# Three full attentions: turned probabilities as the weights of the value products, sums from a ones column, division by token, result turned afterwards

## The reference, cut to what matters

```python
def _L3_xcond_ref(q, k, v, tau, delta, Wq, bq, Wk, bk, Wv, bv, Wo, bo):
    qh = (q @ Wq.T + bq).reshape(B, L, H, E)
    kh = (k @ Wk.T + bk).reshape(B, S, H, E)
    vh = (v @ Wv.T + bv).reshape(B, S, H, E)
    scores = jnp.einsum('blhe,bshe->bhls', qh, kh)
    scores = scores * tau[:, None, None, :] + delta[:, None, None, :]
    a = jax.nn.softmax(scale * scores, axis=-1)
    out = jnp.einsum('bhls,bshd->blhd', a, vh).reshape(B, L, D)
    return out @ Wo.T + bo
...
x = x + _L3_xcond_ref(_layernorm(x, axis=-1), ctx_1024, ctx_1024, condB_tau[:, None], fside_BxS2_0, ...)
```

## Time and profile before

| | us |
|---|---|
| median of 3 runs | 3504.17 (3503.16 to 3506.55) |
| the profiled execution's own time | 3504.71 |
| its span, first to last instruction | 3503.0 |
| TensorE busy | 3144.3 (90%) |
| VectorE busy | 2451.7 (70%) |
| ScalarE busy | 1078.8 (31%) |
| GpSimd busy | 940.4 (27%) |

### The profile page before, as it was taken

How to read it: one execution, slowest core, us unless ns; L and a number is a source line. 1 busy time by engine, 2 the same in 40 slices (tenths; PEclk the granted TensorE clock), 3 DMA queues, 4 the chain that set the end, 5 groups by cost and what they waited for, 6 DMA issues and landing times. The chain is left out here.

```text
span 3503.0 us, 67687 instructions
## 1 busy us (share of the span) xinstructions
PE 3144.3 (90%) x27654; PEld 2380.6 (68%) x27670; DVE 2451.7 (70%) x6457; ACT 1078.8 (31%) x1919; POOL 940.4 (27%) x1000
## 2 busy tenths in 40 slices
PE   5998999897699756577799999999999997999999
PEld 4776766565477623366688888888888885777444
DVE  5787355001577799844688888888888884778666
ACT  3444211221344344444322222222222212444000
POOL 2332000232243200000144434434435343333000
PEclk9999999999799977788799999999999997999999
DMA  3100210343300000021200000000000002010000
GB/s 124 38 26 16 81 50 13 88 115 77 111 26 26 11 1 1 22 68 38 97 1 1 1 1 1 1 1 1 2 1 1 2 1 75 26 38 2 13 19 18
DMA packets 81171, 108.26 MB, mean 31 GB/s; under 512 B 11744, under 2 KB 62176, under 8 KB 80480
## 3 DMA queue, kind: packets, MB, share of 16 engines
q1 hardware_dynamic: 74720, 95.40, 8.3%
q0 software_dynamic: 6144, 8.52, 1.3%
HBM read 87.00 MB, written 16.91 MB: 30 GB/s over the span
## 5 line engine op out<-in xcount | busy, mean ns | idle before, releaser
L2035 POOL TENSOR_TENSOR pk_hisig<-pk_hihot,pk_sigs 128x512 f16<-128x512 f16 x512 | 520.6, 1044 | 668.3 <-DVE pk_hihot L2242 667.4
L2096 PE MATMUL pk_ps<-pk_nt,ew_downT 128*128 128x128 f32 x4096 | 515.5, 279 | 0.0
L2096 PEld LDWEIGHTS pk_ps<-pk_nt,ew_downT 128*128 128x128 f32 x4096 | 479.7, 192 | 15.3 <-issue 15.3
L2137 PE MATMUL pk_ps<-ew_up,pk_act_h 128*128 128x256 f32 x2048 | 450.4, 381 | 0.9 <-DVE pk_act_h L2230 0.9
L2137 PEld LDWEIGHTS pk_ps<-ew_up,pk_act_h 128*128 128x128 f32 x2048 | 388.8, 191 | 53.1 <-issue 1.0
L2043 ACT ACTIVATE pk_act_h<-pk_ps 128x512 f32<-128x512 f32 x256 | 153.0, 597 | 542.3 <-PE pk_ps L2096 542.3
L2243 DVE TENSOR_TENSOR pk_lohot<-pk_iota_h,pk_ps 128x1024 f16<-128x1024 f16 x256 | 312.1, 1219 | 0.0
L568 DVE RECIPROCAL a_rden<-a_ps_o 128x256 f32<-128x256 f32 x96 | 168.4, 1754 | 159.9 <-PE a_ps_o L458 159.9
L557 DVE TENSOR_REDUCE a_mx<-a_ps_s 128x8 f32<-128x1024 f32 x192 | 226.1, 1219 | 54.4 <-PE a_ps_s L432 54.3
L273 ACT ACTIVATE a_pT<-a_ps_t 128x512 f32<-128x512 f32 x384 | 209.0, 599 | 145.8 <-PE a_ps_t L441 145.6
L2416 PE MATMUL mo_ps<-mw_we,mo_xnT 128*128 128x512 f32 x512 | 225.6, 599 | 0.0
(11 more groups left out here) (353 smaller groups left out, 5433.5 us busy)
## 6 DMA issues: line engine op xcount, KB each, us to landing
ro_w<-in_L_W SPq DMA_DIRECT2D x16, 1024.0 KB, 7.1
a_ctx_t<-in_ctxT SPq DMA_DIRECT2D x24, 512.0 KB, 3.8
a_tau<-in_tau SPq DMA_DIRECT2D x24, 256.0 KB, 4.1
a_delta<-in_delta SPq DMA_DIRECT2D x24, 256.0 KB, 4.3
X<-in_x SPq DMA_DIRECT2D x4, 1024.0 KB, 9.5
row_dram<-sh_row SPq DMA_DIRECT2D x8, 512.0 KB, 3.2
sum_dram<-sh_new SPq DMA_DIRECT2D x8, 512.0 KB, 2.9
X<-sum_dram SPq DMA_DIRECT2D x4, 1024.0 KB, 9.6
```

The lines of the kernel that those rows point to most:

```text
L2035: ins = pool.tensor_tensor(hisig[:, buf, n, :, :, :], hi, sig2.broadcast_to([P, TP, 2, ECH]), ALU.mult)
L2096: ins = pe.matmul(hid.bank(f"h{c}")[:, j * P:(j + 1) * P], downT[:, k, e * P:(e + 1) * P], nt[:, s, k, :], start=(k == 0), stop=(k == KC - 1))
L2137: ins = pe.matmul(tail.bank("y")[:, 0:D], act_h[:, s, c, :], up[:, c, :], start=(c == 0), stop=(c == ECH - 1))
```

## The change

In the three attentions `weighted_values` exchanges its operands. The turned probabilities of one head, 128x128, are now the weights, and the head's values with a column of ones behind them, 17 columns, move. There are 16 products a tile in place of 32, into one bank with a row for each token and 17 columns for each head: 16 results and the sum. `divide` takes the reciprocal of 128x16 sums and multiplies with it broadcast over a head's 16 columns, into the new tile `o`, token by feature. Since `output_rows` needs features on partitions, `o` is turned by two transposes (`turn_out`) into one of the two banks `ps_t`, and ScalarE copies them out to `oT` (`out_columns`). These two stand one slot later, between the first m piece and `turn_probs(t, 2)` on TensorE, and between the emptying of the first m piece and `exps(t, 2)` on ScalarE. The two banks are used in turn over five uses a tile instead of four (`use`, `use_out`). The zeros in `v` and the tile `ones` are gone.

```diff
-        v = sb("v", [P, 2, G * HEADS // 2, 3 * DK])
+        v = sb("v", [P, 2, G * HEADS, DK + 1])
...
-        rden = sb("rden", [P, D])
+        rden = sb("rden", [P, HEADS])
+        o = sb("o", [P, 2, D])
...
+        sums = ps_o[:, 0:HEADS * (DK + 1)].rearrange("p (h e) -> p h e", h=HEADS)
+
+        def use(t, j):
+            return 5 * t + j + (j >= 2) - (t >= 1 or j >= 2)
+
+        def use_out(t):
+            return 5 * t + (6 if t < TILES - 1 else 4)
...
+            def out_columns(t, parity):
+                act.wait_ge(t_full, use_out(t) + 1)
+                act.activation(oT[:, parity, :, :], ps_t[use_out(t) % 2][:, 0:D].rearrange("p (k n) -> p k n", k=KC),
+                               ACT.Copy).then_inc(t_taken, 1)
...
                     if more and u == 3:
                         values(g + 1, 1 - s, 0, m)
+                    if not at_start(t, 1):
+                        out_columns(t - 1, (u + 1) % 2)
                     exps(t, 2)
                     exps(t, 3)
...
             def turn_probs(t, parity, j):
                 pe.wait_ge(p_ready, t * 2 + j // 2 + 1)
-                if not (at_start(t, 1) and j < 2):
-                    pe.wait_ge(t_taken, t * 4 + j - 1)
+                if use(t, j) >= 2:
+                    pe.wait_ge(t_taken, use(t, j) - 1)
...
+            def turn_out(t, parity):
+                pe.wait_ge(o_taken, t + 1)
+                pe.wait_ge(t_taken, use_out(t) - 1)
+                for k in range(KC):
+                    ins = pe.transpose(ps_t[use_out(t) % 2][:, k * P:(k + 1) * P], o[:, parity, k * P:(k + 1) * P],
+                                       ident[:, :])
                 ins.then_inc(t_full, 1)
...
-                pe.wait_ge(t_taken, t * 4 + j + 1)
-                at, half = j // 2 * P, j % 2 * DK
+                pe.wait_ge(t_taken, use(t, j) + 1)
                 for c in range(4):
-                    pair = u * HEADS // 2 + 4 * (j // 2) + c
-                    pe.matmul(ps_o[32 * c:32 * c + 32, at:at + P], v[:, s, pair, half:half + 32], pT[:, 4 * j + c, :],
-                              start=(j == 0), stop=(j % 2 == 1), skip_group_check=True)
-                for c in range(4):
-                    ins = pe.matmul(ps_o[32 * c:32 * c + 32, D + at:D + at + P], ones[:, half:half + 32],
-                                    pT[:, 4 * j + c, :], start=False, stop=(j % 2 == 1), skip_group_check=True)
+                    head = 8 * (j // 2) + 2 * c + j % 2
+                    ins = pe.matmul(sums[:, head, :], pT[:, 4 * j + c, :], v[:, s, u * HEADS + head, :], start=True,
+                                    stop=True, skip_group_check=True)
...
             def output_rows(t, parity):
-                pe.wait_ge(o_taken, t + 1)
+                pe.wait_ge(t_taken, use_out(t) + 1)
...
                         else:
                             values(1 - s, 0, m)
+                    if not at_start(t, 1):
+                        turn_out(t - 1, (u + 1) % 2)
                     turn_probs(t, u % 2, 2)
                     turn_probs(t, u % 2, 3)
...
-                dve.reciprocal(rden[:, :], ps_o[:, D:2 * D]).then_inc(den_ready, 1)
+                dve.reciprocal(rden[:, :], sums[:, :, DK]).then_inc(den_ready, 1)
                 if not at_start(t, 2):
-                    dve.wait_ge(y_full, t - 1)
+                    dve.wait_ge(t_full, use_out(t - 2) + 1)
                 dve.wait_ge(den_ready, t + 1)
-                dve.tensor_tensor(oT[:, parity, :, :], ps_o[:, 0:D].rearrange("p (k n) -> p k n", k=KC),
-                                  rden[:, :].rearrange("p (k n) -> p k n", k=KC), ALU.mult).then_inc(o_taken, 1)
+                dve.tensor_tensor(o[:, parity, :].rearrange("p (h e) -> p h e", h=HEADS), sums[:, :, 0:DK],
+                                  rden[:, :].rearrange("p (h a) -> p h a", a=1).broadcast_to([P, HEADS, DK]),
+                                  ALU.mult).then_inc(o_taken, 1)
```

More of the change, by code:

```diff
@@ L171, in attention @@
         bo2 = sb("bo2", [P, D])
-        ones = sb("ones", [P, 3 * DK])
         ctx_t = sb("ctx_t", [P, 2, KC, GT])
@@ L266, in values @@
                 act.wait_ge(v_full, g * 2 + n + 1)
-                pairs = v[:, s, n * HEADS:(n + 1) * HEADS, :].rearrange("p a (b e) -> p a b e", b=3)
-                act.activation(pairs[:, :, 0:3:2, :], src.rearrange("p (a b e) -> p a b e", b=2, e=DK),
-                               ACT.Copy).then_inc(v_taken, 1)
+                heads = v[:, s, n * 2 * HEADS:(n + 1) * 2 * HEADS, 0:DK]
+                act.activation(heads, src.rearrange("p (a e) -> p a e", e=DK), ACT.Copy).then_inc(v_taken, 1)
             def exps(t, j):
-                act.wait_ge(t_full, t * 4 + j + 1)
-                act.activation(pT[:, 4 * j:4 * j + 4, :], ps_t[j % 2][:, :].rearrange("p (h n) -> p h n", h=4),
+                act.wait_ge(t_full, use(t, j) + 1)
+                act.activation(pT[:, 4 * j:4 * j + 4, :],
+                               ps_t[use(t, j) % 2][:, :].rearrange("p (h n) -> p h n", h=4),
                                ACT.Exp).then_inc(t_taken, 1)
+            def out_columns(t, parity):
+                act.wait_ge(t_full, use_out(t) + 1)
+                act.activation(oT[:, parity, :, :], ps_t[use_out(t) % 2][:, 0:D].rearrange("p (k n) -> p k n", k=KC),
+                               ACT.Copy).then_inc(t_taken, 1)
             def outputs(t, parity):
@@ L324, in _ @@
             groups(act, group)
-            for t in (TILES - 2, TILES - 1):
-                outputs(t, t % 2)
+            outputs(TILES - 2, 0)
+            out_columns(TILES - 1, 1)
+            outputs(TILES - 1, 1)
         @block.gpsimd
@@ L437, in turn_probs @@
                 pe.wait_ge(p_ready, t * 2 + j // 2 + 1)
-                if not (at_start(t, 1) and j < 2):
-                    pe.wait_ge(t_taken, t * 4 + j - 1)
+                if use(t, j) >= 2:
+                    pe.wait_ge(t_taken, use(t, j) - 1)
                 for c in range(4):
-                    ins = pe.transpose(ps_t[j % 2][:, c * P:(c + 1) * P], probs[:, parity, j, c, :], ident[:, :])
+                    ins = pe.transpose(ps_t[use(t, j) % 2][:, c * P:(c + 1) * P], probs[:, parity, j, c, :],
+                                       ident[:, :])
+                ins.then_inc(t_full, 1)
+            def turn_out(t, parity):
[3 more added lines that the diff above has]
+                    ins = pe.transpose(ps_t[use_out(t) % 2][:, k * P:(k + 1) * P], o[:, parity, k * P:(k + 1) * P],
+                                       ident[:, :])
                 ins.then_inc(t_full, 1)
@@ L542, in _ @@
                 queries(0, c, s_banks[2 + c])
-            pe.wait_ge(zero_ready, 4)
+            pe.wait_ge(zero_ready, 2)
             scores(0, 0, 0)
             groups(pe, group)
-            for t in (TILES - 2, TILES - 1):
-                pe.wait_ge(y_taken, t)
-                output_rows(t, t % 2)
+            pe.wait_ge(y_taken, TILES - 2)
+            output_rows(TILES - 2, 0)
+            turn_out(TILES - 1, 1)
+            pe.wait_ge(y_taken, TILES - 1)
+            output_rows(TILES - 1, 1)
         @block.vector
@@ L558, in softmax @@
                 if not at_start(t, 2):
-                    dve.wait_ge(t_full, t * 4 - 4)
+                    dve.wait_ge(t_full, use(t - 2, 3) + 1)
                 for n in range(2):
@@ L589, in group @@
                         row_stats(t - 2)
[L591 to L594, removed]
+            dve.memset(v[:, :, :, DK:DK + 1], 1.0).then_inc(zero_ready, 1)
             dve.memset(ones_h[:, :], 1.0 / DK ** 0.5).then_inc(zero_ready, 1)
```

## The result

The changed kernel takes 3850.6 us (median of 4 runs, 3843.6 to 3880.4), the kernel before 3505.0: a ratio of 1.100, interval 1.0975 to 1.1033. Slower was right; 346 us more instead of 192 was not. The profiled execution is the longest of the four, 3880.4 us.

A forecast was written before the change was run, and what follows sets the result against it. TensorE was taken to set the pace, with VectorE binding too in each attention's last group. Three attentions at 57.9 + 6.1 us added 192 us to 3504.2, giving 3696 us, range 3650 to 3765 us.

The forecast's parts named there:

- The sum: All costed terms over three attentions: 57.9 us for groups with m pieces plus 6.1 for the last group, 192 us more.
- turning: Two added transposes of `o` on TensorE at 0.11 us each: +0.22 us a tile, +0.9 a group.
- the new wait: TensorE's fourth `turn_probs` waits for ScalarE's `out_columns`: 0.76, 0.67, 1.52 and 0.67 us by slot, 3.4 a group taken.
- VectorE's short reciprocal: Reciprocal of 16 columns at 0.25 us; VectorE's 1.5 us less a tile costed at nothing, lying beside TensorE's work.
- hand-overs: TensorE's waits at the change to narrow products, in groups with m pieces, should vanish: -0.16 and -0.07, -0.9 us a group.
- the -0.5: At u = 2 `output_rows` no longer waits for the second emptying of the queries: -0.5 us a group.
- the ends: An attention's last tile: TensorE's 0.9 us wait for VectorE's division goes, and the very end gets 0.6 us shorter.
- list of signs: What the profile should show, including TensorE waiting for `a_oT` before the fourth `turn_probs`, some 70 us in all.
- the clock falls: Rival: TensorE's clock drops with 17 columns moving; partly, 66 us more, 3762 us, chance 0.13; fully, 4043 us, chance 0.05.
- the likeliest case: The forecast proper: the costed terms with hand-overs and waits off by a third, 3665 to 3730 us, chance 0.73.
- cheap weight loads: Rival: f32 loads of 128 columns in the value products at 0.040 us a record: 3493 us, faster, chance 0.03.
- the wait is hidden: Rival: TensorE's added wait for `out_columns` costs nothing, so 76 us go: 3620 us, chance 0.06.

The follow-up runs named there:

- 119-column kernel: The changed kernel with each value product's moving operand read seven times over, 119 columns instead of 17: 3692.5 us, ratio 1.0530.
- the turning alone: The kernel before plus two transposes, ScalarE's copy (read by nobody) and the new bank order, with old value products and division: 3590.6 us, ratio 1.024.
- 119-column kernels with and without the wait: The changed kernel with 119 columns moving, 3692.5 us; the same with turn_out and out_columns moved to where their bank is free, 3624.5 us.
- later-turn kernel: The changed kernel with turn_out and out_columns moved behind weighted_values(t, 1) and exps(t, 3), where their bank is free: 3662.8 us, ratio 1.0444.
- new, 34: The changed kernel with each value product's moving operand read twice, 34 columns instead of 17: 3743.8 us, ratio 1.0699.
- new, 68: The changed kernel with each value product's moving operand read four times over, 68 columns instead of 17: 3695.4 us, ratio 1.0538.
- f16 run: The changed kernel with turn_out and out_columns moved to where their bank is free, and pT and v in f16: 3462.2 us, ratio 0.9875.

## Why the prediction was wrong, by its own steps

**The sum was right for a clock that holds.** The 119-column kernel has every term of the sum (products at 0.106 us a record, turning, the new wait, VectorE's short reciprocal) and a clock of 1.00: 3692.5 us against the 3696 predicted. Its 186 us over the kernel before (3506.8 in that comparison) divide nearly as the sum does: the turning alone is 84, the products with what they save are the other 102. By the prediction's terms turning is (0.22 x 4 + 3.4) x 7 x 3 less the first tiles, and some 0.6 a tile in the last groups: 95 us; the products with hand-overs, the -0.5 and the ends come to about 97. So one part came out 11 us lower and the other 5 higher, and that the whole fits to 4 us is in part luck. By slots it is as close: a group of four tiles takes 8.24 us more than before (8.4 predicted), and the slots take 11.9, 9.3, 12.7 and 11.8 us. Two readings in it are off without a cost: 1.91 - 1.77 and 0.97 - 0.88 are 0.14 and 0.09, not 0.16 and 0.07, with the same sum; and 1.01 us for 32 records is 32 ns each, while 27 ns is what they take inside a half (8 from 243.38 to 243.60) without the hand-over.

**The new wait** was sized well, a little too long. At u = 2 the fourth `turn_probs` should have started at 238.81 + 0.44 = 239.25 and started at 240.65: 1.40 us, 1.52 predicted. At u = 3 it is 258.99 - 258.44 = 0.55 against 0.67. The trace counts less, 1.25 and 0.40, since it counts from the modelled end of the last transpose, and so its total is 42.1 us where the prediction's list of signs has some 70. The 119-column kernels with and without the wait differ by 0.69, 0.55, 1.45 and 0.60 us in the four kinds of slot (0.76, 0.67, 1.52 and 0.67 predicted) and by 0.27 in the last group (0.4 predicted).

**VectorE** was costed rightly at nothing: its reciprocal is 0.26 us (0.25 predicted), and it waited for the value products at all 96 tiles, 484.5 us in total:

```profile
DVE a_rden L593 <- PE a_ps_o L479: 484.5, 96, 9.2
```

**The step that failed** is the rival "the clock falls", taken out of the likeliest case with "the fall that I looked at follows real idleness ... and a slot has full-width work between the halves", and given 0.13 for a partial fall. It was what happened, and it cost 3850.6 - 3692.5 = 158 us. "Real idleness" was not needed, as the falls of the later-turn kernel show, and in the last group, by the prediction's own account, the halves stand back to back with no work between them. The rival's size was wrong too: 33 slots with 2 us each, 66 us, where only slots with transposes as m piece and the last groups were counted. The slots that the wait strikes hardest, u = 2, were left out and fell most, and u = 0 and 3 fell as well. There were 67 falls of 6.1 us on average, and at half speed such a fall costs up to 3 us. Half of the 405 us is 203, against 187 us between the two profiled executions of the 17-column and the 119-column kernel (3880.4 and 3692.9). The wait was priced by its length alone, and the products by theirs; the two were never laid side by side.

**What the runs show in its place** is a cause with two parts:

| medians, us | wait before the products | turned later, no wait |
|---|---|---|
| old products (32 columns of weights, 128 moving) | 3590.6 | not run |
| new, 17 columns moving | 3850.6 | 3662.8 |
| new, 34 | 3743.8 | not run |
| new, 68 | 3695.4 | not run |
| new, 119 | 3692.5 | 3624.5 |

The falls of the clock after the first tile of each attention, counted by the slot in which they begin:

| | u = 0 | 1 | 2 | 3 | last groups | us at 1.2 GHz |
|---|---|---|---|---|---|---|
| 17, wait | 11 | 16 | 18 | 10 | 12 | 405 |
| 17, turned later | 0 | 9 | 0 | 0 | 9 | 98 |
| 34, wait | 0 | 5 | 10 | 0 | 3 | 96 |
| 68, wait | 0 | 0 | 4 | 0 | 0 | 14 |
| 119, with and without the wait; old products, with and without the turning | 0 | 0 | 0 | 0 | 0 | 0 |

With 119 columns the wait costs 68 us, which is its own length: 3.3 us a group by the slots above, about 69 us in 21 groups. With 17 it costs 188: the other 120 are the clock. Without the wait, narrow products cost 38 us of clock; with the old products the wait costs none. So of the 346 us, some 84 are turning with its wait, 102 the weight loads, 38 the clock of narrow products by themselves, and 120 the clock of narrow products behind a pause.

**The rival "cheap weight loads"** is refuted for f32 by 1.70 us a half; the f16 run shows how it would have looked. The rival "the wait is hidden" is refuted by the timeline. **The rules of the Trainium skill.** The record at full clock takes 0.106 us with 17 columns moving and 1.78 / 16 = 0.11 with 119, in f32. The Trainium skill, TensorE: Matmul & The Clock Gate, section Back-to-back issue gap, has 81 ns for a matmul that moves 128 columns, which does not fit these records. Transposes: in the later-turn kernel only slots at u = 1, where transposes lie between the two halves, and last groups fell, but with 119 columns the window shows 1.00 with the same transposes, and no run isolates them. The Trainium skill's rule on transposes (same page, section Part 4: PE-mode transpose), as the prediction read it, pointed at these slots and missed the others: with the wait, slots with u = 0, 2 and 3 fell too.

**Open.** Whether the pause must stand beside the value products, or would bring the clock down from anywhere in a slot, was not tried. Nor was the wait taken in pieces. The later turn moves the two transposes together with the wait, so no run has one without the other; that the pause counts rests on the falls with 34 and 68 columns, which favour the slots with the long pause.

## What to carry to other kernels

Before an operand swap, count weight loads by their columns: here 32 loads of 128 columns at 0.106 us took the place of 64 of 32 columns at 0.027 (0.032 with the hand-over), and nothing on VectorE could pay for it. When a change makes TensorE's records narrow and also adds a wait, price the two together, and look at the granted clock first; if the clock sags with a full list, moving surplus columns beside the loads, or moving the wait away, is a quick test, and was worth 155 and 188 us here. A copy that frees a bank should be asked for later, as in the later turn; whether putting it ahead of other emptying on its engine does as well was not tried.

## What the runs showed of the hardware that was not expected

The clock can fall with no hole in TensorE's list at the time: at 242.4 us it did so inside a half of the value products that had begun at 241.12, after a pause of only 1.25 us, and it stayed down through 13.6 us of value products, full-width products, scores and transposes. In the later-turn kernel it did so with no pause at all in the microseconds before (328.5 us, TensorE busy throughout). Streaming 7 times the columns beside an f32 weight load of 128 columns cost nothing (3.51 us for a half and the m piece behind it, with 17 and with 119) and kept the clock at 1.00. An f16 load of 128 columns with its 17-column product took 0.026 us against 0.106 in f32.
